# A two-layer transformer kernel: first score maxima between the matmuls of the last projections, and base products interleaved with query and key products in layer 1

## The chip, the cores and the metric

The program runs on one core of one Trainium2 chip. The metric is the device time of one execution in microseconds (us). The engines are named as in the profile: PE (TensorE, matmuls), PEld (its weight loads), DVE (VectorE), ACT (ScalarE), POOL (GpSimd) and SP (SyncE, which here issues all DMA transfers).

## The reference, cut to what matters

Two layers, each with an attention and a feed-forward part that both read the same layer-normed input; everything is f32, x is 2 x 1024 x 512.

```python
xn = layernorm(x)
x = x + L0_attn(xn) + L0_ffn(xn)      # L0_attn: 32 query heads of 16, ONE key and value head, biases
xn = layernorm(x)
x = x + L1_attn(xn) + L1_ffn(xn)      # L1_attn: 32 query heads, 8 key/value heads, rotary, causal
...
def L1_ffn(x):
    w = two largest of softmax(x @ W_router.T), renormalised   # 8 experts
    h = einsum('td,erd->ter', x, lora_A)                        # rank 16
    return x @ W_base.T + b_base + 2 * einsum('ter,eor,te->to', h, lora_B, w)
```

## The kernel before, in words

The 2048 tokens are 16 tiles of 128 (`TT`) or 4 chunks of 512 (`NCH`); the 512 features are 4 blocks of 128 (`KC`). `acc` holds x, `xnT` the transposed normed input. PSUM has eight banks of 128 x 512 (`bank(i)`). All cross-engine order is written out by hand with semaphores: each engine runs its instructions strictly in the order in which the code lists them.

Each layer has, after its feed-forward work, three stages.

**Projections.** 20 products, numbered i = 5c + m: for each chunk c the four query blocks m = 0 to 3 and the key block m = 4 (in layer 0 keys and values together, 32 columns). One product is 4 f32 matmuls of 128 x 512, which the profile counts as 8 records (L1248). ACT copies each product out of PSUM (`q32_ready`) and DVE (in layer 1 both, with the rotary embedding: `rope`, `remainder`, `lowest` on DVE, L954 to L980; `high_roped`, `middle` on ACT) splits it into 2 f32r or 3 bf16 parts. SP stores the parts to memory (`store_parts`, L388) and reads them back in the layout of an attention group (`load_slot`, L400 to L416, 12 transfers into one of 3 slots). In layer 1 the values are 16 further products of 128 x 128, one for each token tile (L1260), after the 20.

**First maxima.** Attention runs over 16 groups of 4 heads. Its softmax subtracts the row maximum, so every group needs a maxima pass: for each item of `max_blocks` PE computes a scores tile into a pair of banks (3-4 or 5-6 in turn; L1346 in layer 0, L1340 and L1343 in layer 1) and DVE reduces it (L1012, L1015); behind the maxima of a chunk a transpose (L1336) hands the chunk's maxima over, negated (L1024, L1026), and SP puts them into the slot as rows (`max_rows`). The maxima of a group run beside the attention of the group before it. Group 0 has no group before it: its first 23 items (`pieces(0, 0, cut(0))`, L1455) run alone, between the projections and the attention.

**Attention.** For each group: scores (L1431, L1427) to PSUM, exponentials on ACT (L752), products with the values (L1401), with the rest of this group's and the first of the next group's maxima in between.

In layer 1 the feed-forward work precedes the projections: `lora_in` (L1184), the gate on DVE (L899 to L933), then `base_product(t)` (L1202, 8 records, into one of 6 banks), the transposed weighted LoRA activations (`hwT`, L1214 on PE, L667 on ACT) and `lora_product(t)` (L1206, 2 records), and DVE adds the bank to `acc` (L937). The projections wait for the last of these (L1226).

## Time and profile before

| | us |
|---|---|
| three runs: lowest, median, highest | 2013.52, 2013.70, 2018.43 |
| the profiled execution's own time | 2015.05 |
| its span on the core | 2013.5 |
| PE busy | 1910.6 (95%) |
| DVE busy | 1379.6 (69%) |
| ACT busy | 1090.0 (54%) |
| mean granted TensorE clock | 0.975 of 2.4 GHz |

Busy times are sums over instructions; matmuls are pipelined and their ends are modelled, so PE can be shown as busy while it waits little or runs at half clock. The share of the whole says little about one stage; the stages are read from stretches of the trace.

### The profile page before, as it was taken

How to read it: one execution, taken by the hardware profiler on the slowest of the kernel's cores; microseconds unless marked ns; L12 is line 12 of the kernel's file. 1: busy time of each engine (PE TensorE's matmuls, PEld its weight loads, DVE VectorE, ACT ScalarE, POOL GpSimd, SP SyncE). 2: the span in 40 equal slices, each digit the busy share in tenths (PEclk: the TensorE clock that was granted, in tenths of full speed). 3: DMA queues.
4: the chain of work that ended last, by engine and by line, in shares of the span. 5: the costliest groups of instructions: out<-in, count | busy, mean ns of one | idle time of the engine just before them, and what ended most of it. 6: DMA issues, size and time to landing. Idle time of an engine off the chain costs nothing.

```text
span 2013.5 us, 29092 instructions
## 1 busy us (share of the span) xinstructions
PE 1910.6 (95%) x10864; PEld 977.8 (49%) x10864; DVE 1379.6 (69%) x1719; ACT 1090.0 (54%) x2177; POOL 231.4 (11%) x606
## 2 busy tenths in 40 slices
PE   6999999998999999999999999999699999999998
PEld 5888887633333333333334346644433333333446
DVE  6554544417899999999897836429677777777733
ACT  3221212232778888788776853204257777677662
POOL 1000000000000001000000100000023433332330
PEclk9999999996999999999999999999879999999999
DMA  6010100042113111122112001002412212212102
GB/s 210 1 48 1 43 1 1 12 143 65 30 37 82 32 31 33 31 49 39 30 31 57 7 7 56 1 0 79 118 25 51 48 32 51 46 34 51 30 10 87
DMA packets 79211, 87.52 MB, mean 43 GB/s; under 512 B 19072, under 2 KB 52864, under 8 KB 79072
## 3 DMA queue, kind: packets, MB, share of 16 engines
q1 hardware_dynamic: 79072, 85.67, 16.9%
q8 instruction: 87, 1.43, 0.3%
q14 instruction: 52, 0.43, 0.1%
HBM read 55.20 MB, written 20.71 MB: 38 GB/s over the span
## 4 chain that ended last, share of the span: by engine, by line
PE 78%; DVE 8%; ACT 7%; SPq 3%; issue 2%; DMA 1%; POOL 0%; DVEq 0%; POOLq 0%; ACTq 0%
PE ps L1401 18%; PE ps L1431 11%; PE ps L1108 8%; PE ps L1109 7%; PE ps L1110 7%; ACT arena L752 6%; PE ps L1427 6%; PE ps L1340 5%; PE ps L1248 4%; PE ps L1346 4%; PE ps L1202 3%; DVE arena L1012 2%; SPq L444 2%; SPq L442 1%; DMA slots<-arena 1%
## 5 line engine op out<-in xcount | busy, mean ns | idle before, releaser
L752 ACT ACTIVATE arena<-ps 128x512 f32<-128x512 f32 (+3 forms) x1792 | 867.4, 557 | 367.5 <-PE ps L1431 188.1
L1012 DVE TENSOR_REDUCE arena<-ps 128x1 f32<-128x1024 f32 (+3 forms) x768 | 855.2, 1153 | 141.8 <-PE ps L1343 66.9
L1401 PE MATMUL ps<-arena 128*17 128x512 f32 (+3 forms) x3584 | 434.9, 557 | 1.0 <-ACT arena L752 0.6
L1346 PE MATMUL ps<-slots 48*128 48x512 f32 x1024 | 410.2, 477 | 9.7 <-DVE arena L1012 8.5
L1431 PE MATMUL ps<-slots 50*128 50x512 f32 x1024 | 384.6, 455 | 22.2 <-ACT arena L752 13.8
L1431 PEld LDWEIGHTS ps<-slots 50*128 50x128 f32 x1024 | 171.2, 187 | 319.8 <-ACT arena L752 273.4
L1427 PE MATMUL ps<-slots 98*128 98x512 bf16 (+3 forms) x768 | 209.3, 331 | 9.7 <-DMA slots<-arena 6.3
L1340 PE MATMUL ps<-slots 96*128 96x512 bf16 (+3 forms) x768 | 199.4, 336 | 16.3 <-DVE arena L1015 8.4
L1346 PEld LDWEIGHTS ps<-slots 48*128 48x128 f32 x1024 | 172.4, 191 | 58.2 <-DVE arena L1012 33.0
L575 POOL TENSOR_SCALAR_AFFINE_SELECT arena<-arena 128x128 f32<-128x128 f32 x512 | 144.4, 292 | 346.6 <-ACT arena L752 338.7
L636 ACT ACTIVATE xn<-ps 128x512 f32<-128x512 f32 (+1 forms) x44 | 26.3, 598 | 260.7 <-PE ps L1110 260.7
L851 DVE TENSOR_TENSOR xn<-xn,ps 128x512 f32<-128x512 f32 (+1 forms) x44 | 30.2, 687 | 166.4 <-ACT xn L636 166.4
L1108 PE MATMUL ps<-x_hi,w_hi 128*128 128x512 f32 (+1 forms) x352 | 138.7, 394 | 5.0 <-DVE x_lo L833 5.0
L1109 PE MATMUL ps<-x_lo,w_hi 128*128 128x512 f32 (+1 forms) x352 | 138.2, 393 | 0.0
L1110 PE MATMUL ps<-x_hi,w_lo 128*128 128x512 f32 (+1 forms) x352 | 138.1, 392 | 0.0
L1427 PEld LDWEIGHTS ps<-slots 98*128 98x128 bf16 x768 | 62.1, 98 | 152.8 <-ACT arena L752 104.6
L1015 DVE TENSOR_REDUCE arena<-ps 128x4 f32<-128x512 f32 (+2 forms) x96 | 97.6, 1044 | 45.0 <-PE ps L1343 45.0
L1401 PEld LDWEIGHTS ps<-arena 128*17 128x17 f32 x3584 | 59.6, 95 | 111.7 <-ACT arena L752 79.3
L1248 PE MATMUL ps<-xnT,w_q 128*128 128x512 f32 x256 | 112.4, 595 | 0.9 <-DVE acc L937 0.9
L1343 PE MATMUL ps<-mask_qk,identb 128*128 128x128 bf16 x512 | 107.7, 224 | 0.0
L1340 PEld LDWEIGHTS ps<-slots 96*128 96x128 bf16 x768 | 70.9, 99 | 71.7 <-DVE arena L1015 19.1
L541 POOL COPY arena<-v_all 128x136 f32<-128x136 f32 x32 | 9.3, 298 | 671.2 <-PE ps L1401 558.2
(127 smaller groups left out, 1851.8 us busy)
## 6 DMA issues: line engine op xcount, KB each, us to landing
slots<-qparts SPq DMA_DIRECT2D x96, 128.0 KB, 3.5
qparts<-arena SPq DMA_DIRECT2D x32, 256.0 KB
xnT<-arena SPq DMA_DIRECT2D x256, 32.0 KB
slots<-qparts SPq DMA_DIRECT2D x96, 64.0 KB, 3.2
qparts<-arena SPq DMA_DIRECT2D x48, 128.0 KB
slots<-qparts SPq DMA_DIRECT2D x32, 192.0 KB, 3.6
w_raw<-in_wgu SPq DMA_DIRECT2D x20, 256.0 KB, 3.2
acc<-in_x SPq DMA_DIRECT2D x4, 1024.0 KB, 7.8
```

The source lines that it names most:

```text
L575: pool.affine_select(out=p, in_=p, compare_op=ALU.is_ge, fill=0.0, base=0, pattern=[[1, P]], channel_multiplier=-1).then_inc(S["p_masked"], 1)
L752: act.activation(prob[local % P_RING][:, q0:CH], bank(local % SP_RING)[:, q0:CH], ACT.Exp, scale=SCALE).then_inc(S["p_ready"], 1)
L1012: dve.tensor_reduce(maxes[c][:, h[0] * TPC + qt:h[0] * TPC + qt + 1], src[:, 0:w], AX_X, ALU.max).then_inc(S["x_done"], 1)
L1108: pe.matmul(out_, hi_w, hi_x, start=start, stop=False)
L1109: pe.matmul(out_, hi_w, lo_x, start=False, stop=False)
L1110: return pe.matmul(out_, lo_w, hi_x, start=False, stop=stop)
L1248: last = pe.matmul(bank(m)[0:wide, :], w, xnT[:, k, c * CH:(c + 1) * CH], start=(k == 0), stop=(k == KC - 1))
L1340: last = pe.matmul(dst[:, k0:k1], q_slot1[u][0:ROWS[1], c, h, qt * P:(qt + 1) * P], k_slot1[u][0:ROWS[1], k0:k1], start=True, stop=k1 < w)
L1346: last = pe.matmul(dst[:, k0:k1], q_slot[u][r:r + ROWS[0], c, h % 2, qt * P:(qt + 1) * P].bitcast(F32R), k_slot[u][r:r + ROWS[0], k0:k1].b ...
L1401: mm = pe.matmul(bank(7)[32 * h:32 * h + DH + 1, q0:CH], v_slot[n % SLOTS][:, kt, :], prob[idx % P_RING][:, q0:CH], start=(kt == 0), stop= ...
L1427: mm = pe.matmul(bank(slot)[:, q0:CH], k_slot1[u][0:ROWS[1] + MROWS, kt * P:(kt + 1) * P], q_slot1[u][0:ROWS[1] + MROWS, c, h, q0:CH], sta ...
L1431: mm = pe.matmul(bank(slot)[:, q0:CH], k_slot[u][r:r + ROWS[0] + MROWS, kt * P:(kt + 1) * P].bitcast(F32R), q_slot[u][r:r + ROWS[0] + MROW ...
```

## The change

It moves work and adds no arithmetic.

1. Layer 0: the 23 first items of the maxima pass are issued on PE one by one between the matmuls of products 12 to 19 (after the 1st, 2nd and 3rd of the four matmuls of each), and DVE reduces them between its other steps of the projections. Products now rotate over banks 0 to 2, value transposes use bank 7 alone.
2. Layer 1: the weights of the feed-forward part are in another place of the arena and so load later (`load_ffn1` waits for `y2_ready`); the base, LoRA and projection work is one sequence: product 0, base 0, product 1, base 1, product 2, base 2, products 3 and 4, and then for each token tile t a transpose of `hw`, LoRA product t, base product t + 3 and query or key product t + 5. DVE and ACT run the rotary and the splits in that order (`ROPES`). Base products rotate over banks 3 to 6, the transposes and the value products share bank 7.
3. Layer 1: the 16 value products come last, and behind each stand one or two of the first 23 items of the maxima pass.
4. SP: stores are unrolled; slot 0 is loaded once its own memory is prepared; slot 1 is loaded before store 13 (layer 0) or 17 (layer 1); the maxima rows of group 0 are written before store 18 (layer 0) or after the last store (layer 1). POOL prepares slots 1 and 2 of layer 1 only after the last LoRA product. ACT waits for the last split instead of the last store before the attention.

```diff
+HWT_RING = 8
+ROPES = [[0, 1], [2], [3, 4], [5], [6, 7], [8], [9, 10], [11], [12], [13], [14], [15], [16], [17], [18], [19]]
+FIRST_MAX_AT = 12
+ROWS_AT = [18, 20]
+LOAD_AT = [13, 17]
...
+def maxima_in_product(i, k, count):
+
+    j = 3 * (i - FIRST_MAX_AT) + k
+    return range(j, j + 1) if i >= FIRST_MAX_AT and k < 3 and j < count else range(0)
+
+
+def maxima_behind_value(t, count):
+    return range(t * count // TT, (t + 1) * count // TT)
+
+
+def product_behind(t):
+
+    return range(KC + 1 + t, KC + 2 + t) if KC + 1 + t < NCH * (KC + 1) else range(0)
...
+                for i in range(QC * NQ, NCH * NQ):
+                    if i == LOAD_AT[l]:
+                        sp.wait_ge(S["v_slot_ready"], SLOTS)
+                        for n in range(1, SLOTS - 1):
+                            load_slot(l, n)
+                    if i == ROWS_AT[l]:
+                        max_rows(l, 0, 0, 0)
+                    store_parts(l, i)
...
-                    sp.wait_ge(L[0]["o_copied"], GROUPS * QC + 1)
+                    sp.wait_ge(L[0]["y2_ready"], TT)
                     load_ffn1()
-                    sp.wait_ge(L[0]["y2_ready"], TT)
...
+                        if u == 1:
+                            pool.wait_ge(S["b_ready"], TT)
...
+                    for i in range(NQ):
+                        whole(i)
+                    copy_hwT(0)
+                    copied = NQ
+                    for t in range(TT):
+                        if t < TT - 1:
+                            copy_hwT(t + 1)
+                        for r in ROPES[t]:
+                            while copied < NCH * NQ and copied < NQ + t and copied <= r + 2:
+                                whole(copied)
+                                copied += 1
+                            split(r)
+                    for t in range(TT):
+                        copy_v(t)
+                        if t < HI_LAG + 1:
+                            split(NCH * NQ + t)
...
+                if l:
+                    for t in range(TT):
+                        for r in ROPES[t][:-1]:
+                            roped(r)
+                        base_evac(t)
+                        roped(ROPES[t][-1])
+                    for t in range(TT):
+                        for j in maxima_behind_value(t, count):
+                            maximum(j, *first[j])
+                        if t < HI_LAG + 1:
+                            roped(NCH * NQ + t)
+                else:
+                    for i in range(NCH * NQ):
+                        for k in range(KC):
+                            for j in maxima_in_product(i, k, count):
+                                maximum(j, *first[j])
+                            if k == 0 and i:
+                                lower(i - 1)
+                        if i >= NQ and i % NQ == 0:
+                            take_v(i // NQ - 1)
...
+                    if i >= 3 and k0 == 0:
+                        pe.wait_ge(S["q32_ready"], i - 2)
...
+                            if piece[0] == 0 and piece[-2]:
+                                pe.wait_ge(S["slot_in"][0], 16 * 12)
+                                pe.wait_ge(*((S["b_evac"], TT) if l else (S["y_evac"], TT * len(ROUNDS) + 1)))
+                            max_piece(*piece)
...
+                    for t in range(TT):
+                        if t < TT - 1:
+                            transpose_hw(t + 1)
+                        lora_product(t)
+                        if t < TT - 3:
+                            base_product(t + 3)
+                        for i in product_behind(t):
+                            product(i)
+                    for t in range(TT):
+                        value_product(t)
+                        first_maxima(maxima_behind_value(t, count))
```

`roped(i)` is `rope(i)`, `remainder(i - 2)` and `lowest(i - 3)`; `split(i)` is `high_roped(i - 2)` and `middle(i - 3)`; `whole(i)` is ACT's copy of product i.

**PE, layer 0, at the end of the projections, before.** The last key product (i = 19), the value transposes (`ident,arena 128x32`) and the first maxima items (`ps<-slots`):

```order
L1248 MATMUL ps<-xnT,w_kv 32x512 [waits q32_ready_0]
L1248 MATMUL ps<-xnT,w_kv 32x512 x3
L1235 MATMUL ps<-ident,arena 128x32 [waits v_done_0,q32_ready_0]
L1235 MATMUL ps<-ident,arena 128x32 x3
L1346 MATMUL ps<-slots 128x512 [waits v_done_0,q32_ready_0,v_slot_ready_0,slot_in0_0]
L1346 MATMUL ps<-slots 128x512 x3
L1346 MATMUL ps<-slots 128x512 [waits x_done_0]
```

**The same engine now, in product 12** (`xnT,w_q` is a quarter of the product, `ps<-slots` twice is one item):

```order
L1435 MATMUL ps<-xnT,w_q 128x512 [waits q32_ready_0]
L1362 MATMUL ps<-slots 128x512 [waits y_evac_0,slot_in0_0]
L1362 MATMUL ps<-slots 128x512
L1435 MATMUL ps<-xnT,w_q 128x512
L1362 MATMUL ps<-slots 128x512 x2
L1435 MATMUL ps<-xnT,w_q 128x512
L1362 MATMUL ps<-slots 128x512 [waits x_done_0]
```

The wait for slot 0 (`slot_in0_0`) stood behind all products and their value transposes; now it stands behind the first quarter of product 12, and three quarters of that product and seven products are queued behind it.

**PE, layer 1, the feed-forward part before** (`ident,arena` is the transpose for `hwT`, L1206 the LoRA product, `arena,xnT` a base product):

```order
L1214 MATMUL ps<-ident,arena 128x128 [waits hwT_sb_1,hw_done_1]
L1206 MATMUL ps<-arena 128x512 [waits hwT_sb_1]
L1202 MATMUL ps<-arena,xnT 128x512 [waits b_evac_1]
L1202 MATMUL ps<-arena,xnT 128x512 x3
L1214 MATMUL ps<-ident,arena 128x128 [waits hwT_sb_1,hw_done_1]
```

**Now**, one step of the loop over t, with a query product in it:

```order
L1279 MATMUL ps<-ident,arena 128x128 [waits hwT_sb_1,hw_done_1]
L1283 MATMUL ps<-arena 128x512 [waits hwT_sb_1]
L1273 MATMUL ps<-arena,xnT 128x512 [waits b_evac_1]
L1273 MATMUL ps<-arena,xnT 128x512 x3
L1435 MATMUL ps<-xnT,w_q 128x512 [waits q32_ready_1]
L1435 MATMUL ps<-xnT,w_q 128x512 x3
```

The 20 products stood behind the last of these steps; now 15 of them stand one in each step, and five ahead of step 0.

**PE, layer 1, now, behind the last LoRA product** (`w_kv,xnT` is a value product, `ps<-slots1` and the mask product make up an item):

```order
L1283 MATMUL ps<-arena 128x512 [waits hwT_sb_1]
L1423 MATMUL ps<-w_kv,xnT 128x128 [waits hwT_sb_1]
L1423 MATMUL ps<-w_kv,xnT 128x128 x3
L1356 MATMUL ps<-slots1 128x128 [waits b_evac_1,slot_in0_1]
L1359 MATMUL ps<-mask_qk,identb 128x128
L1356 MATMUL ps<-slots1 128x128
L1359 MATMUL ps<-mask_qk,identb 128x128
```

Two more such pairs end item 0, and the next value product follows, which waits for ACT's copy of the one before out of bank 7 (`v_done_1`). Before, the 16 value products came behind each other and all 23 items behind the last of them.

## Rows read from the trace of the kernel before

**Rows 1.** The page, part 1: busy time and share of each engine.
```profile
PE 1910.6 (95%) x10864; PEld 977.8 (49%) x10864; DVE 1379.6 (69%) x1719; ACT 1090.0 (54%) x2177; POOL 231.4 (11%) x606
```
**Rows 2.** The chain of waits, 440 to 500: start us, us, what.
```profile
448.37 11.86 PE ps L1248 x27
...
465.85 1.24 DVE arena L1012
467.13 1.23 PE ps L1346 x2
```
**Rows 3.** Stretches: us, busy (x instructions) by engine, PEclk, DMA share, GB/s.
```profile
core 0: us, PE busy (x) PEld busy (x) DVE busy (x) ACT busy (x) POOL busy (x), PEclk, DMA share, GB/s
433.69:462.42 28.73, 28.73 (x69) 10.68 (x67) 5.66 (x9) 10.10 (x16) 0.00 (x0) 1.00 0.55 159
462.42:465.12 2.70, 0.43 (x5) 0.35 (x5) 0.81 (x2) 1.25 (x2) 0.31 (x2) 1.00 0.50 140
465.12:493.22 28.10, 23.86 (x45) 10.47 (x46) 24.96 (x23) 1.28 (x1) 0.48 (x2) 0.53 0.25 51
493.22:504.10 10.88, 10.88 (x41) 4.54 (x40) 8.54 (x8) 6.52 (x12) 0.00 (x0) 0.50 0.00 1
...
1350.30:1421.90 71.60, 71.58 (x184) 33.12 (x184) 64.66 (x119) 27.78 (x50) 2.73 (x3) 1.00 0.30 81
1421.90:1434.16 12.26, 0.00 (x0) 0.00 (x1) 12.03 (x22) 6.15 (x12) 0.00 (x0) 0.66 0.46 138
1434.16:1449.30 15.14, 14.37 (x105) 14.21 (x106) 0.51 (x1) 3.95 (x15) 0.33 (x2) 0.83 0.56 161
1449.30:1472.09 22.79, 18.44 (x81) 6.78 (x82) 20.49 (x23) 0.00 (x0) 0.45 (x2) 0.66 0.00 0
1472.09:1480.20 8.11, 7.75 (x39) 4.12 (x41) 5.41 (x8) 3.81 (x8) 2.04 (x7) 0.50 0.06 13
```
**Rows 4.** Timeline, SP's queue around the load of slot 0 in layer 0.
```profile
428.48 0.81 SPq L388 DMA_DIRECT2D kparts<-arena  x2
430.89 0.35 SPq L411 DMA_DIRECT2D slots<-qparts  x1
...
435.95 0.42 SPq L416 DMA_DIRECT2D slots<-kparts  x1
```
**Rows 5.** DMA issues, 428 to 446: KB each, median us to landing.
```profile
slots<-kparts SPq DMA_DIRECT2D x2, 64.0 KB, 3.2
```
**Rows 6.** The chain of waits, 1270 to 1352: six base products, then one LoRA and one base product.
```profile
1278.19 20.87 PE ps L1202 x48
...
1302.60 3.43 PE ps L1202 x8
1306.14 0.86 PE ps L1206 x2
```
**Rows 7.** Timeline: two f32r matmuls of 512 columns in turn at full clock.
```profile
1235.37 0.39 PE L1110 MATMUL ps<-wo_hi,xo_lo 128*128 128x512 f32 x1
1235.59 0.39 PE L1108 MATMUL ps<-wo_hi,xo_hi 128*128 128x512 f32 x1
```
**Rows 8.** Timeline, ACT's copies that end a chunk of a group, layers 0 and 1.
```profile
520.49 0.60 ACT L743 ACTIVATE arena<-ps 128x512 f32<-128x512 f32 x1
541.85 0.60 ACT L743 ACTIVATE arena<-ps 128x512 f32<-128x512 f32 x1
...
1488.15 0.59 ACT L743 ACTIVATE arena<-ps 128x512 f32<-128x512 f32 x1
1507.64 0.59 ACT L743 ACTIVATE arena<-ps 128x512 f32<-128x512 f32 x1
1518.22 0.59 ACT L743 ACTIVATE arena<-ps 128x512 f32<-128x512 f32 x1
```
**Rows 9.** Layer 1's first maxima, DVE's groups from 1449.2 to 1472.3: busy us, mean ns, idle before.
```profile
L1012 DVE TENSOR_REDUCE arena<-ps 128x1 f32<-128x640 f32 (+3 forms) x15 | 14.5, 1006 | 1.6 <-PE ps L1343 1.4
L1015 DVE TENSOR_REDUCE arena<-ps 128x2 f32<-128x768 f32 (+3 forms) x6 | 5.9, 1043 | 15.3 <-PE ps L1343 15.3
```

More of the change, by code:

```diff
@@ L664, in _ @@
                     act.activation(egap, gap, ACT.Exp).then_inc(S["egap_done"], 1)
-                    for t in range(TT):
-                        act.wait_ge(S["hwT_ready"], t + 1)
-                        act.activation(hwT[:, t, :], bank(t % 2)[:, 0:P], ACT.Copy).then_inc(S["hwT_sb"], 1)
                 if l == 0:
@@ L688, in middle, with whole @@
                     act.activation(part1[m][:, 1, :], rest[m], ACT.Copy).then_inc(S["mid_done"], 1)
-                for i in range(NCH * NQ):
+                def whole(i):
                     c, m = divmod(i, NQ)
-                    rows = 2 * DH if (m == KC and l == 0) else P
                     if c:
@@ L706, in _ @@
[L706 to L712 removed]
+                        high(i, src, bias if m < KC else bias_kv[0:DH, 0:1])
+                        act.activation(q32[m][0:rows, :], src[0:rows, :], ACT.Identity, bias=bias).then_inc(S["q32_ready"], 1)
+                    else:
+                        act.activation(q32[m], src, ACT.Copy).then_inc(S["q32_ready"], 1)
@@ L1204, in lora_product, with transpose_hw @@
+                    def transpose_hw(t):
+                        pe.wait_ge(S["hw_done"], t + 1)
+                        if t:
+                            pe.wait_ge(S["hwT_sb"], t)
+                        pe.transpose(bank(7)[:, 0:P], hw[:, t, :], ident[:, :]).then_inc(S["hwT_ready"], 1)
                     def lora_product(t):
                         pe.wait_ge(S["hwT_sb"], t + 1)
-                        pe.matmul(bank(2 + t % 6), hwT[:, t, :], w_lb, start=False, stop=True).then_inc(S["b_ready"], 1)
@@ L1253, in _ @@
-                if l == 0:
-                    transpose_v(NCH - 1)
-                for t in range(TT if l else 0):
-                    if t >= 3:
-                        pe.wait_ge(S["v_done"], t - 2)
-                    for k in range(KC):
-                        last = pe.matmul(bank(5 + t % 3)[:, 0:kw], xnT[:, k, t * P:(t + 1) * P], w_kv[:, k, kw:2 * kw],
-                                         start=(k == 0), stop=(k == KC - 1))
-                    last.then_inc(S["v_ready"], 1)
-                pe.wait_ge(S["v_done"], V_STEPS[l])
@@ L1264, in _ @@
-                pe.wait_ge(S["q32_ready"], NCH * NQ)
+                        pe.matmul(bank(3 + t % 4), hwT[:, t % HWT_RING, :], w_lb, start=False, stop=True).then_inc(S["b_ready"], 1)
+                pe.wait_ge(S["wp_in"], 16 * (6 if l == 0 else 3))
                 causal = l == 1
```

235 lines of the change are left out of this document (120 added, 115 removed).

## The prediction

> **What bounds the kernel now.** I read the page's busy times first, then the chain of waits, then stretches of the trace, and last the timelines at the places that the change touches. PE is busy 95% of the span and DVE 69% [rows 1], so PE is the bound on the whole; the whole, though, hides two stages in which it is not. The chain of waits shows the first: from 465.85 it goes DVE, PE, DVE, PE in pieces of 1.24 and 1.23 us [rows 2]. That is group 0's first maxima pass in layer 0, 23 items in 28.10 us, with PE at 0.53 of its clock and nothing for it to do but this [rows 3]. The same pass in layer 1 takes 22.79 us at a clock of 0.66, and ahead of it lie 12.26 us in which PE has no instruction at all and 15.14 us for 13 of the 16 value products [rows 3]. The 12.26 us are DVE's: it is busy 12.03 of them with the rotary and splits, which it could not finish beside the 20 products, and ACT cannot copy values out before them. The reader is to see in the table of stretches one column after the other: who is busy, and what clock PE was granted.
>
> The granted clock matters too. It is 1.00 to 465, 0.50 in 493.22 to 504.10, when attention has already begun and PE is busy throughout, and 0.50 again in 1472.09 to 1480.20 [rows 3]. What that costs is read from ACT's copies: in layer 0 a chunk lasts 21.36 us [rows 8], four of its 32 exponentials come before the copy, so from a group's first score to its first copy a warm PE needs about 21.4 + 2.7 = 24.1 us; here it took 520.49 - 493.22 = 27.3. Loss 3.2 us. In layer 1 the short chunk lasts 10.58 us for 16 exponentials [rows 8], so 10.6 + 2.6 = 13.2 against 1488.15 - 1472.09 = 16.1: loss 2.9 us.
>
> **The sum, layer 0.** Until product 12 nothing on PE changes but bank numbers; a product waits for the copy of the one three before, which is two products (6.9 us) old, so I cost it nothing. Product 12 starts at 433.69, and today attention starts 59.5 us later, at 493.22 [rows 3]. Now:
> - The first quarter of product 12, 0.86 us (a product is 3.43 us [rows 6], as all of 128 x 512 in f32), to 434.55.
> - A new wait, for slot 0. Its 12 transfers are issued after the stores of product 9, from 430.89 on, the last at 435.95, and land 3.2 us after issue [rows 4, 5], so near 439.4. The change lets it start no earlier. PE stands for about 5 us, with seven and three quarter products queued behind it. This wait lies on the path.
> - 31 quarters, 26.6 us, and one set of value transposes, 0.9.
> - 22 items of two f32r matmuls at full clock, 0.22 to 0.23 us apart [rows 7], so 0.45 each, and a transpose: 10.0 us. DVE needs 1.27 us an item (28.10 us less start, over 22) and 0.6 for a split, 4.4 us for each product with three items; PE needs 3.43 + 1.35 = 4.8. So DVE keeps up by 0.4 us a product and costs nothing; if its items took 1.4 us it would be the bound.
> - The clock. 5 us of idle PE are more than it had before the fall at the end of the products today (the three lines of 462 to 493 [rows 3]), so it falls. With dense work behind, the nearest case is 1434.16 to 1449.30: mean 0.83, so a third of 15.14 us at half clock. I take 4 us at half, 2.0 lost; bounds 0 and 5.
>
> That is 439.4 + 26.6 + 0.9 + 10.0 + 2.0 = 478.9 for the end of product 19, and as today 2.7 us [rows 3] of copy, transposes, split and slot copy: attention starts at 481.6 instead of 493.2. **Gain 11.6 us.** Those 2.7 us with 0.43 of PE work are the same as today's, and the clock fell behind them today; I therefore take attention to start cold as now and add nothing. Warm, it would add 3.2.
>
> **The sum, layer 1.** The later weight loads cost nothing: they are issued where today's rotary tables are, ahead of them, some 8 us before the first LoRA matmul needs the small two; were they late by a few us, all of it would be on the path. From 1278.19, the start of the base products [rows 6], PE has 36 products of 3.43 (123.5), 16 LoRA products of 0.86 [rows 6] (13.8) and 16 transposes of 0.1 (1.7), and a new wait at step 0: product 4 ends, ACT copies it and the first transpose, about 1.1 us. End 1418.3. Today's 20 products end within 1 us of that, since they were PE-bound too: the interleaving alone gains nothing on PE. What it buys is DVE's time. The 20 rotary sets cost DVE 64.66 + 12.03 us [rows 3], 3.8 each, and now have 125 us to lie in, beside 16 additions of 0.7. In a step of 7.8 us (0.1 + 0.86 + 3.43 + 3.43) DVE does 0.7 + 3.8, or 8.3 in the four steps with two sets; it is never more than a step behind. So at 1418.3 only set 19 and the last splits remain: the last addition to 1419.3, set 19 to 1423.2. The 12.26 us are gone.
>
> Then the value products and the maxima. PE has 16 x 0.9 = 14.4 us of values (13 in 15.14 us at 0.83 of the clock [rows 3]) and maxima of 18.44 us at 0.66, so at most 12.2 warm [rows 3]. DVE has 14.5 + 5.9 + 1.2 (the last falls outside those rows) [rows 9] + 0.6 for the transposed item, 22.2, and 3.2 of leftover splits, from 1423.2: 1448.6 at the earliest. The two are close. At the start ACT's second value copy is queued behind a split that waits for DVE in set 19; PE stands 1421.4 to 1423.5, and about 3 us more for DVE until 1431. The clock probably falls there, but while PE waits for DVE a slow PE costs little; I add 1 us. PE ends about one item ahead of DVE: attention starts at 1449.7 instead of 1472.1. **Gain 22.4 us.** By then PE has run almost without a gap, nearest to the rows before 1421.90 at 1.00, so I take attention to start warm: **2.9 us** more.
>
> SP: slot 1's 12 transfers (5.5 us by the pace of [rows 4]) move ahead of store 13, where no one waits for that store but SP; in layer 1 ahead of store 17, after POOL's memsets behind the last LoRA product, so 1420 to 1425.5, and stores 17 to 19 follow to 1432.5, the maxima rows to about 1438. All are ahead of 1449. The cover is 11 us; a later start of these would go on the path.
>
> 11.6 + 22.4 + 2.9 = 36.9. The profiled execution took 2015.05; that gives 1978.2. It stood 1.35 above the median of the runs, 2013.70, so against the median **1976.8**, which I round to 1977. Bounds: layer 0 from 8.6 (5 lost to the clock) to 16.8 (no loss, warm start); layer 1 from 17 (3 us of further waits, 2.4 of clock, cold start) to 27. Together 25.6 to 43.8: 1970 to 1988.
>
> **Rivals.**
> - *The clock does not hold behind the values.* In the first maxima pass today it fell although PE was busy, and stayed at half (0.66 over 1449.30 to 1472.09 [rows 3]). The small waits for DVE and for the one bank 7 would do it again: PE would need 28.8 + 24.4 = 53 us for values and maxima, attention would start at 1471 and cold. Layer 1 gains 1, the whole 12.6: **2001**. Against it: a PE at half clock would be busy without a gap, and such stretches with f32 work got the clock back (1434.16 to 1449.30). The Trainium skill, "TensorE: Matmul & The Clock Gate", section "A second HAM failure mode: psum-queue depth-cycling", says that small pauses between groups of matmuls that cycle through PSUM banks make the clock oscillate; by that rule this change does harm, and the sum would be 2001. The trace agrees for one dense mix only. Chance 0.11.
> - *Layer 0 gives little.* Slot 0 lands later, among the stores, or DVE becomes the bound between the quarters. Gain 2 instead of 11.6: **1986 to 1988**. Against it: the queue was the same in rows 4. Chance 0.11.
> - *Slower.* ACT runs strictly in order: its copy for the next `hwT` stands behind a split that waits for DVE, whose set stands behind the addition that waits for the LoRA product, which waits for that copy. If this closes into one chain, a step lasts 0.86 + 0.7 + two sets of 3.8 + three ACT copies of 0.6 = 11.0 us instead of 7.8, 15 steps give 48 us, and the time is 2013.7 - 36.9 + 48 = **2025**. It decides from a step of 10.3 us on. Against it: only four steps have two sets, and `high_roped` lags by two products. Chance 0.03.
> - *It doesn't do what it says*: the waits leave values and maxima in series as today: within 0.3%, 0.02.
>
> **How the numbers follow.** The forecast has 0.73, the rivals 0.11, 0.11, 0.03 and 0.02. 1977 is the likeliest case. The range takes in its bounds and the second rival, 1969 to 1990; what is left out is the first rival, the last two and a tail, under 0.2. A difference of 0.3% (6 us) is about what a measurement of this kernel can tell from none. Faster 0.95, same 0.02, slower 0.03.
>
> **What would show it.** In layer 0: a wait of 4 to 6 us on PE for a slot transfer behind the first quarter of product 12, a clock of 0.5 behind it, DVE's reductions 1.6 us apart and not 1.27, and attention starting near 482. In layer 1: steps of 7.8 us, products ending near 1407 (all of layer 1 lies 11.6 earlier), no PE gap of 12 us, attention near 1438 and its first copy 13 us later. It is wrong if attention in layer 0 starts after 488, if steps last over 8.5 us, or if values and maxima take over 35 us.

## The result, and the profile after

| | before | changed |
|---|---|---|
| median of 20 runs, us | 2019.38 | 1996.54 |
| lowest, highest | 2006.74, 2031.62 | 1984.01, 2013.84 |
| profiled execution, us | 2015.05 | 2006.20 |
| its span | 2013.5 | 2004.5 |

The ratio of the changed kernel to the kernel before is 0.9895, with a 95% interval of 0.9872 to 0.9919: faster by 1.05%, some 21 us. One of the changed kernel's 20 runs (2013.84) was in the slower of the two states that a kernel shows, and the ratio leaves it out. The forecast was 1977 against 2013.70, a ratio of 0.982. The direction was right, the size was not, and the time lies outside the range.

The page's busy times hardly move (compare [rows 1]); the work is the same:

```profile
PE 1914.6 (96%) x10864; PEld 975.3 (49%) x10864; DVE 1379.2 (69%) x1719; ACT 1088.6 (54%) x2177; POOL 232.4 (12%) x606
```

What the change touched is in the stretches. These are the changed kernel's, with the columns of [rows 3]: products to the first quarter of product 12, PE's stop, items and products at half clock, the same at full clock, the step into attention and its first 11 us; then layer 1: base, LoRA and product steps, first values, values with items, and the first 8 us of attention.

```profile
core 0: us, PE busy (x) PEld busy (x) DVE busy (x) ACT busy (x) POOL busy (x), PEclk, DMA share, GB/s
390.49:434.45 43.96, 43.96 (x107) 17.28 (x105) 8.93 (x15) 14.66 (x24) 3.00 (x3) 1.00 0.38 113
434.45:439.02 4.57, 0.00 (x1) 0.00 (x0) 0.00 (x0) 0.50 (x1) 0.00 (x0) 0.92 0.71 146
439.02:462.40 23.38, 23.38 (x30) 7.34 (x30) 8.54 (x8) 2.53 (x4) 0.00 (x0) 0.50 0.42 105
462.40:495.90 33.50, 33.50 (x82) 10.80 (x81) 23.60 (x25) 6.31 (x10) 0.00 (x0) 1.00 0.27 73
495.90:498.66 2.76, 0.44 (x5) 0.32 (x4) 0.81 (x2) 1.42 (x3) 0.35 (x2) 1.00 0.47 145
498.66:509.54 10.88, 10.01 (x46) 4.11 (x46) 7.45 (x7) 7.88 (x15) 0.44 (x2) 0.69 0.05 15
1294.18:1434.43 140.25, 139.41 (x337) 61.90 (x337) 92.80 (x231) 33.40 (x72) 0.95 (x1) 1.00 0.17 50
1434.43:1437.95 3.52, 3.23 (x33) 2.86 (x31) 3.45 (x7) 1.83 (x4) 1.84 (x2) 1.00 0.24 72
1437.95:1467.43 29.48, 26.50 (x180) 20.38 (x179) 24.71 (x31) 6.41 (x19) 0.53 (x3) 0.88 0.32 92
1467.43:1475.54 8.11, 6.75 (x55) 3.44 (x53) 6.54 (x9) 5.00 (x12) 3.18 (x12) 1.00 0.12 33
```

Three things are to be seen. PE stands 4.57 us in layer 0, the wait that the forecast named. Behind it the clock is at half for 23.38 us although PE is busy in all of them. And even at full clock 33.50 us pass until the products end at 495.90; the first scores come at 498.66, where 481.6 was forecast and 493.22 was the time before. The forecast had called itself wrong if they came after 488. In layer 1 the 140.25 us of the interleaved steps are as forecast, and the gap of 12.26 us in which PE had nothing to do is gone.

ACT's copies tell what each stage got. First copy of layer 0 and of layer 1 in the changed kernel, to be held against 520.49 and 1488.15 in [rows 8]:

```profile
524.64 0.60 ACT L797 ACTIVATE arena<-ps 128x512 f32<-128x512 f32 x1
1481.13 0.59 ACT L797 ACTIVATE arena<-ps 128x512 f32<-128x512 f32 x1
```

With the last copy of layer 0 (1219.64 before, 1235.67 now) and that of layer 1 (1977.71 and 1970.21) the span splits into five pieces:

| us | before | changed | gain |
|---|---|---|---|
| start to first copy of layer 0 | 520.5 | 524.6 | -4.1 |
| to the last copy of layer 0 | 699.1 | 711.0 | -11.9 |
| to the first copy of layer 1 ("layer 1's stage" below) | 268.5 | 245.5 | 23.0 |
| to the last copy of layer 1 | 489.6 | 489.1 | 0.5 |
| to the end | 35.8 | 34.3 | 1.5 |

So layer 1 brought all of the gain and layer 0's part lost. The 11.9 us in the second line are no work of the change. Nearly all chunks last 21.4 us in both kernels; in the changed kernel's profile two of the last six last 38.9 and 32.7, with the clock at half for 41 us between 1073 and 1114, where before they last 28.9 and 25.9. Three kernels below have the changed kernel's layer 0 order, and the first of these chunks lasts 28.9, 28.9 and 30.2 in them. Of all fourteen below eleven have 28.3 to 30.2 for it and three have 38.9 (one of the eleven then has 35.4 and 38.2 for the next two). This alone makes single executions differ by 10 us or more. It is probably a good part of why the profiled pair differs by 8.9 us and the medians by 22.8, and it is why I read stages below rather than whole times. The 20 runs of the kernel before spread over 1.2%, more than the 0.3% that the forecast took from three.

Layer 1's stage has a spread of its own. Eleven of the profiled kernels have the changed kernel's layer 1 order: their stage takes 241.3 to 245.5 us. Up to 2.6 us of this lies ahead of the sequence of products (56.0 to 58.6 us from the last copy of layer 0 to its first matmul). From that first matmul to the first copy they take 185.3 to 187.0 us: 186.9 or 187.0 in the six whose clock fell for 6.8 us among the values and maxima, 185.3 to 185.5 in the five where it fell for 3.4 us or not at all. So this fall costs 1.6 us, and it is this narrower time that I compare between layer 1 orders.

### The profile page after: what moved, and what is told of

Read it like the earlier page. It is cut to its first block, busy times and chain, and to the rows that moved or that the text cites. A ratio compares the mean times of both kernels' runs of the same rounds, so it can differ in the third digit from the quotient of the medians.

```text
span 2004.5 us, 28840 instructions
## 1 busy us (share of the span) xinstructions
PE 1914.6 (96%) x10864; PEld 975.3 (49%) x10864; DVE 1379.2 (69%) x1719; ACT 1088.6 (54%) x2177; POOL 232.4 (12%) x606
## 4 chain that ended last, share of the span: by engine, by line
PE 81%; ACT 7%; DVE 4%; SPq 4%; issue 2%; DMA 2%; POOL 0%; DVEq 0%; POOLq 0%; ACTq 0%; PEldq 0%
PE ps L1498 19%; PE ps L1528 11%; PE ps L1179 8%; PE ps L1180 7%; PE ps L1181 7%; PE ps L1435 7%; ACT arena L806 6%; PE ps L1524 6%; PE ps L1356 5%; PE ps L1362 4%; PE ps L1273 3%; SPq L468 2%; SPq L466 1%; DMA slots<-arena 1%; DVE arena L1043 1%
## 5 line engine op out<-in xcount | busy, mean ns | idle before, releaser
L1362 PE MATMUL ps<-slots 48*128 48x512 f32 x1024 | 409.7, 474 | 8.8 <-DMA slots<-kparts 4.6
L1356 PE MATMUL ps<-slots 96*128 96x512 bf16 (+3 forms) x768 | 193.6, 328 | 13.8 <-DVE arena L1046 7.7
L1362 PEld LDWEIGHTS ps<-slots 48*128 48x128 f32 x1024 | 171.8, 190 | 66.7 <-DVE arena L1043 22.9
L1435 PE MATMUL ps<-xnT,w_q 128*128 128x512 f32 x256 | 125.5, 629 | 0.4 <-ACT arena L632 0.4
```

The lines of the kernel that those rows point to most:

```text
L1356: last = pe.matmul(dst[:, k0:k1], q_slot1[u][0:ROWS[1], c, h, qt * P:(qt + 1) * P], k_slot1[u][0:ROWS[1], k0:k1], start=True, stop=k1 < w)
L1362: last = pe.matmul(dst[:, k0:k1], q_slot[u][r:r + ROWS[0], c, h % 2, qt * P:(qt + 1) * P].bitcast(F32R), k_slot[u][r:r + ROWS[0], k0:k1].b ...
L1435: last = pe.matmul(bank(i % 3)[0:wide, :], w, xnT[:, k, c * CH:(c + 1) * CH], start=(k == 0), stop=(k == KC - 1))
```

## Experiments

All times from the trace are microseconds from the span's start. The first product starts within 0.7 us of 390.3 in every kernel, so ends of the products and first copies of layer 0 can be compared as they stand, to 1 us.

### One part alone

The changed kernel with layer 0's items behind the products again:

```diff
-    j = 3 * (i - FIRST_MAX_AT) + k
-    return range(j, j + 1) if i >= FIRST_MAX_AT and k < 3 and j < count else range(0)
+    return range(0)
...
                     transpose_v(NCH - 1)
+                    first_maxima(range(count))
```

> Undoes the layer 0 part: the 23 first items stand behind all 20 products again, on PE and DVE; layer 1 as changed. Theory: layer 0's part gains nothing or loses (first copy of attention 524.64 in the changed kernel, 520.49 before), and the whole gain is layer 1's. Then the first copy of layer 0 is near 520.5 again, from the first product of layer 1's sequence to its first copy 187 us as in the changed kernel (210 before), and the run is 23 to 27 us below the kernel before, a few us below the changed one. Rival: layer 0's part does gain some 10 us on the median and only the profiled execution hid it; then this kernel is slower than the changed one by that.

Measured: ratio 0.9893 (0.983 to 0.9956), against the changed kernel's 0.9895; first copies at 517.83 and 1460.38, layer 1's stage 245.4. So the layer 0 part brings nothing that the ratio can tell: taken out, the gain stays, within an interval of some 13 us to either side. The profiles are sharper: with the layer 0 part the first copy comes 6.8 us later. (Against the kernel before it was 4.1; there the clock stayed at half until 504.2, here until 499.3.) The pass itself is as in [rows 3], the second and third stretch here being the maxima and the start of attention:

```profile
390.00:462.00 72.00, 71.84 (x174) 27.97 (x172) 14.95 (x24) 24.09 (x39) 3.00 (x3) 1.00 0.50 142
462.00:491.70 29.70, 24.19 (x49) 10.94 (x50) 25.73 (x25) 1.89 (x3) 0.79 (x3) 0.55 0.08 28
491.70:505.00 13.30, 12.99 (x63) 5.78 (x61) 10.91 (x10) 9.43 (x18) 0.00 (x0) 0.71 0.00 1
```

### Layer 0: the clock

First the stop is taken away, by starting when slot 0 has landed:

```diff
-FIRST_MAX_AT = 12
+FIRST_MAX_AT = 14
-    j = 3 * (i - FIRST_MAX_AT) + k
-    return range(j, j + 1) if i >= FIRST_MAX_AT and k < 3 and j < count else range(0)
+    j = 4 * (i - FIRST_MAX_AT) + k
+    return range(j, j + 1) if i >= FIRST_MAX_AT and j < count else range(0)
```

(`ROWS_AT` for layer 0 follows to 19.)

> Starts the items one by one at product 14 instead of 12, one behind each of the four quarters, so that slot 0 has landed (439.0) before PE reaches its wait (441.4). Theory: the clock fell for the 4.6 us in which PE stood for slot 0; without them it stays at 1.00 through the products. With items of 0.66 us and quarters of 1.05 us next to them: 440.6 + 6 products 20.6 + 22 items at 0.45 + 23 x 0.41 for the switches + 0.7 = 481 for the end of the products, first scores 484, first copy 508, 12 us before the kernel before. Rival: the alternation itself brings the clock down to 0.5; then the products end at 493 or later and the first copy is after 518.

```profile
390.68:441.56 50.88, 50.88 (x123) 20.09 (x121) 10.30 (x17) 17.25 (x28) 3.00 (x3) 1.00 0.43 119
441.56:481.10 39.54, 38.59 (x96) 12.61 (x95) 30.59 (x31) 7.64 (x13) 0.00 (x0) 1.00 0.43 118
```

The clock is 1.00 through the same alternation, the products end at 480.1 (481 expected; the last 1.0 us of the second stretch is PE's wait behind them), the first scores come at 483.91. The first copy was at 512.59, later than the 508 expected, since the clock fell in the step into attention and stayed at half for 17 us. Ratio 0.982 (0.9757 to 0.9882), median 1978.4.

Then the stop is put back without items behind it (`pe.wait_ge(S["slot_in"][0], 16 * 12)` after the first quarter of product 12, items from 14 on):

> The start at 14, with the changed kernel's wait for slot 0 put back behind the first quarter of product 12; between the wait and the items lie one and three quarter products without items. PE idles 4.5 us again and the clock falls near 438.5. If the half clock lasts as long whatever follows, it comes back at 462, 24 us later as in the changed kernel, and the products end near 497. If it was the alternating work that kept it down, the plain f32 products bring it back sooner, by 450, and the products end near 490. If idling isn't what brings it down, the clock stays at 1.00 and they end at 485.5.

PE's row behind the stop, and the stretches from it on:

```profile
438.32 8.73 PE L1435 MATMUL ps<-xnT,w_q 128*128 128x512 f32 x14 [4.69 <-DMA slots<-kparts]
```

```profile
439.00:446.00 7.00, 7.00 (x12) 2.83 (x11) 0.69 (x1) 1.27 (x2) 0.00 (x0) 0.69 0.32 118
446.00:486.50 40.50, 40.50 (x100) 12.94 (x98) 30.26 (x31) 7.59 (x12) 0.00 (x0) 1.00 0.38 98
```

The clock did fall, for 6.8 us by the trace's clock record (436.5 to 443.3, 1.8 us of it still in the stop), and was back before the first item at 448.0; the products ended at 486.5, a little earlier than the 490 expected of a quick recovery. The same stop with items directly behind it had cost 23.9 us of half clock by the same record (438.3 to 462.2). So the stop brings the clock down, and the items behind it keep it down. The changed kernel's layer 0 order is in three more of the kernels below: there the half clock lasted 23.9, 23.9 and 13.7 us, so this is a habit of the order and not of one execution. The short recovery with plain products was profiled once.

How short a stop is enough? The start at 13 has one:

```diff
-FIRST_MAX_AT = 14
+FIRST_MAX_AT = 13
```

> The start one by one with four items a product, at product 13 instead of 14: PE reaches the wait for slot 0 at 438.0, and the last transfer lands at 439.0, so PE stands 1 us. It tells whether so short a stop already costs the clock. Theory: it took 4.6 us of idle PE before; 1 us is hidden, the clock stays at 1.00, and the products end at 481, as with the start at 14. Rival: the clock falls, and behind it the items keep it at half for 24 us; the end is near 492.

```profile
437.40:438.92 1.52, 0.01 (x2) 0.01 (x1) 0.00 (x0) 0.50 (x1) 0.00 (x0) 1.00 0.52 142
438.92:440.40 1.48, 1.48 (x4) 0.59 (x4) 0.72 (x1) 0.00 (x0) 0.00 (x0) 1.00 0.52 184
440.40:495.00 54.60, 54.60 (x76) 16.77 (x75) 24.99 (x26) 5.04 (x8) 0.00 (x0) 0.50 0.25 69
```

I had expected nothing of it. The stop was 1.5 us, the clock fell 1.9 us behind its end, and PE then worked 54.6 us at half clock, busy all the time; the products ended at 506.2, later than even the rival's 492, the first copy came at 539.31, and the run took 2022.4. Two kernels tell whether the stop did this. One has the same order with the first item two quarters later (`j = 4 * (i - 14) + k + 2`), so that PE doesn't stop; the other has the wait alone at product 13 and the items from 14 on.

> One item behind each quarter as in the start at 13, but the first behind the third quarter of product 13 (439.7), when slot 0 has landed (439.0), so PE doesn't stop. In the start at 13 PE stood 1.0 us, the clock fell at 440 and stayed at half for 55 us. If that stop of 1.0 us was the cause, the clock here is 1.00 to the end of the products, near 481. If the items cost the clock when they begin this early, or by chance, it falls here too and the end is after 490.

> The start at 14 with PE's wait for slot 0 put behind the first quarter of product 13, where it lasts 1.0 us; behind it three plain quarters before the first item. If a stop of 1.0 us is enough to bring the clock down, it falls near 440 here too; if the plain quarters then bring it back it is up again by 450 and the end is at 484 to 486, if the items keep it down for long the end is after 490. If three plain quarters behind the stop are enough for it not to fall, the end is at 482.

Without the stop, items from 439.89 to the end of the products:

```profile
439.89:480.30 40.41, 40.38 (x100) 13.21 (x99) 30.88 (x31) 7.57 (x12) 0.00 (x0) 1.00 0.41 117
```

With the stop and plain quarters behind it, the stop, the quarters, the items:

```profile
437.21:438.52 1.31, 0.00 (x1) 0.00 (x1) 0.69 (x1) 0.49 (x1) 0.00 (x0) 1.00 0.47 117
438.52:442.27 3.75, 3.75 (x9) 1.20 (x9) 0.00 (x0) 0.82 (x2) 0.00 (x0) 1.00 0.52 186
442.27:480.80 38.53, 38.53 (x96) 12.61 (x95) 30.26 (x31) 6.75 (x11) 0.00 (x0) 1.00 0.40 107
```

Both hold 1.00 to the end of the products, at 480.3 and 480.8 (481 and 482 expected). So neither the early items nor a short stop alone cost the clock; the short stop with items behind it did. Each of the three was profiled once, and the stop without items was 0.2 us shorter, so whether it would each time stays open.

In both kernels the clock then fell in the step into attention and stayed at half for 20.5 us: first copies 513.41 and 514.78, though their first scores came at 483.06 and 484.64. Every profiled kernel has the clock at half somewhere in this step, for 6.8 to 20.5 us in most, and the time from first scores to first copy is 25.4 to 30.4 us with it. First copies therefore carry some 5 us of chance that first scores do not.

### Layer 0: what an item costs

The chain of waits of the changed kernel at full clock, an item (L1362) and a quarter of a product (L1435) in turn:

```profile
469.54 0.66 PE ps L1362 x2
470.20 1.05 PE ps L1435 x2
```

I had taken 0.45 and 0.86. Both are 0.2 us longer, 0.41 for each item. Two more runs tell the number format from the shape, on the order of the start at 14. In the first the items multiply 128 rows, in the second they are f32 like the products but keep their 48 rows.

```diff
+                        if j < count:
+                            last = pe.matmul(dst[:, k0:k1], k_slot[u][:, 0:P].bitcast(F32R),
+                                             k_slot[u][:, k0:k1].bitcast(F32R), start=True, stop=True)
+                        else:
```

> As the start at product 14 one by one, but the 23 first items multiply 128 rows (all rows of the slot's keys with themselves, in place of 48 rows of queries and keys), still f32r; so group 0's first maxima are of other numbers and the row sums of group 0 differ. It tells what makes a quarter 1.05 instead of 0.86 us and an item 0.66 instead of 0.45. If it is the change of row geometry (48 rows at an offset after 128 rows at 0), the quarters take 0.86, the items 0.44 and the products end near 472. If it is the change of number format (f32 to f32r and back), nothing changes: 1.05 and 0.66, end near 480.

The chain, first behind the 32-column key product, then behind a 128-column query product:

```profile
444.74 0.67 PE ps L1362 x2
445.40 0.97 PE ps L1439 x2
446.38 0.66 PE ps L1362 x2
447.04 0.86 PE ps L1439 x2
447.90 0.46 PE ps L1362 x2
448.36 0.86 PE ps L1439 x2
```

```diff
+                        t = F32 if j < count else F32R
-                        last = pe.matmul(dst[:, k0:k1], q_slot[u][r:r + ROWS[0], c, h % 2, qt * P:(qt + 1) * P].bitcast(F32R),
+                        last = pe.matmul(dst[:, k0:k1], q_slot[u][r:r + ROWS[0], c, h % 2, qt * P:(qt + 1) * P].bitcast(t),
...
```

> As the start at 14 one by one, but the 23 first items are f32 matmuls (4 records' worth of time: 2 x 0.86 us instead of 2 x 0.22), on the same 48 rows. If the format change costs, there is none here: quarter 0.86, item 1.72, 2.6 us for both, products end near 500. If the row geometry costs, the quarter stays at 1.05 and the item is 1.93: 3.0 us for both, products end near 509.

```profile
452.20 1.05 PE ps L1436 x2
453.25 1.91 PE ps L1363 x4
```

Format is out: items in f32 leave the quarter at 1.05 and take 1.91, 0.19 above 4 x 0.43, and the products end at 507.7 (509 expected of shape, 500 of format). Shape decides: with 128 rows against 128 x 128 weights the extra vanishes at the row where the products turn from 32 to 128 columns, 0.86 and 0.46, and f32r changes with f32 for nothing (with the 32-column products it stays, so the products ended at 474.4 and not at 472). The timelines show how: in the changed kernel (first two lines) the weight load behind a change starts together with its matmul; with items of 128 rows (third line) it starts at 446.65, under the item before, for the quarter that starts at 447.04.

```profile
468.42 0.30 PEld L1435 LDWEIGHTS ps<-xnT,w_q 128*128 128x128 f32 x2 [0.37 <-issue]
468.42 1.12 PE L1435 MATMUL ps<-xnT,w_q 128*128 128x512 f32 x2
446.65 0.42 PEld L1439 LDWEIGHTS ps<-xnT,w_q 128*128 128x128 f32 x2
```

The Trainium skill, "TensorEngine Tiling (Array Packing)", section "Key Properties", has the rule: a change of tiling mode drains TensorE. The trace agrees with it by the late weight load and by the price: 48 rows against 128, or 32 columns against 128, cost 0.1 to 0.2 us each way. I had not weighed it in the prediction.

Fewer changes, then: items in pairs behind the second and fourth quarter (`return range(j, min(j + 2, count)) if i >= FIRST_MAX_AT and k % 2`, with `j = 4 * (i - 14) + k - 1`).

> As the start at product 14, but the items stand in pairs behind the second and the fourth quarter of a product: 12 places instead of 23. If each change between a quarter and items costs PE 0.2 us, in both directions, this saves 11 x 0.41 = 4.5 us against the start at 14 one by one: products end near 476.5, first copy 503.5. If DVE decides (5.6 us of reductions and split for a product, two items in a row 2.5 us), nothing is saved and PE waits for DVE in the middle of the pairs.

```profile
457.27 1.91 PE ps L1435 x4
459.18 0.67 PE ps L1362 x4
459.85 1.91 PE ps L1435 x4
461.76 1.26 PE ps L1362 x4
```

The first scores come at 476.77, 7.1 us before those of the start at 14 one by one (6.2 if one takes off that the first product starts 0.9 us earlier here), where 4.5 were expected; first copy 503.6, as expected. The last product ends at 473.1, the last item behind it at 473.8. **Median 1973.6, ratio 0.9775 (0.9728 to 0.9821).** The surprise is the pair of 0.67 us: four matmuls in the time of two and a change. The heads stand in the order 2, 0, 3, 1, so the two of a pair read slot rows from 64 and from 0. (Every second pair takes 1.26, since its second item waits for DVE: DVE gets through four reductions and a split in 5.75 us, 2.9 for a pair, where PE alone would come round in 2.6.)

```diff
-        return [(h,) for h in (2, 0, 3, 1)]
+        return [(h,) for h in ((2, 0, 3, 1) if causal else (2, 3, 0, 1))]
```

> The pairs at 14, with layer 0's heads taken in the order 2, 3, 0, 1 instead of 2, 0, 3, 1, so that both items of a pair read slot rows at the same offset (64 and 64, 0 and 0) instead of at 64 and 0. With the pairs at 14 a pair whose banks are free takes 0.67 us for four matmuls of 512 columns, of which each alone takes 0.22. Theory: matmuls in the two halves of the rows run beside each other, two at a time; in the same rows they take 4 x 0.22 + 0.22 = 1.1 us, and the products end up to 2.6 us later (six of the twelve pairs are held by DVE anyway). Rival: 0.67 is how the ends of matmuls are modelled; then it stays at 0.67.

```profile
457.60 1.11 PE ps L1362 x4
458.71 1.91 PE ps L1435 x4
```

1.11 to 1.14 us for each of the first nine pairs, as the theory had it: four matmuls in a row where the two row halves had worked beside each other. The products end at 474.9, 1.8 us later than with the pairs at 14. The order of heads holds for all of layer 0, and its chunks now last 22.5 us instead of 21.4. The one run took 2047.4; some 35 us of the loss are the 32 chunks, and much of the rest falls where the clock was at half, for 51 us from 479 on and for 61 us from 1131 on. Whether the order of heads has to do with these falls was not tested.

### Layer 1: which part of it

Values in one piece and the items behind them, the steps interleaved as changed (on PE `first_maxima(range(count))` behind the loop over `value_product(t)`, on DVE the last `roped` ahead of all maxima):

> Layer 1 with the base and projection steps interleaved as changed, but the 16 value products in one piece and the 23 items behind them, as before. Theory: of the 23 us that layer 1 gained, the interleaving gives what DVE's rotary backlog cost (12.3 us of PE idle) and the overlap of values and maxima the rest. The values take 15 us, the maxima 22.8 as before (DVE and a clock of 0.5 to 0.66), so from the first product of layer 1's sequence to its first copy 187 + 8 (5 in series, 3 for the cold start) = 195 us. Rival: the maxima are DVE-bound either way, and it is no more than 190.

Layer 1's stage was 263.8 us, 18.4 more than the changed kernel's, and 205.3 us from first product to first copy; ratio 1.0022 (0.9987 to 1.0058). Neither theory had that. PE's rows show it: each value product now waits for ACT's copy out of the one bank 7, most of them 1.53 us apart, and the 16 took 27.7 us (the kernel before had three banks for them).

```profile
1437.03 1.16 PE L1422 MATMUL ps<-w_kv,xnT 128*128 128x128 f32 x8 [0.38 <-ACT v_all L750]
1438.57 1.16 PE L1422 MATMUL ps<-w_kv,xnT 128*128 128x128 f32 x8 [0.37 <-ACT v_all L750]
```

So the run undid one thing and laid bare another. The same with four value banks in turn:

```diff
+V_BANKS = [7, 0, 1, 2]
...
-                        last = pe.matmul(bank(7)[:, 0:kw], xnT[:, k, t * P:(t + 1) * P], w_kv[:, k, kw:2 * kw],
+                        last = pe.matmul(bank(V_BANKS[t % 4])[:, 0:kw], xnT[:, k, t * P:(t + 1) * P], w_kv[:, k, kw:2 * kw],
```

> Layer 1's values in one piece and the 23 items behind them, as in the run with the maxima in series, but with the values in four banks in turn (7, 0, 1, 2), so that they needn't wait for ACT's copy of bank 7. There the 16 values took 27.7 us. Theory: half of that run's loss of 18 us was this bank; now the values take 16 us and the stage from the last copy of layer 0 to the first of layer 1 is 264 - 11 = 253 us, still 8 above the changed kernel's 245.4. Rival: DVE's remaining rotary sets hold ACT's copies, and it is 258 or more.

Stage 251.6, where 253 was expected, and 193.0 us from first product to first copy: the single bank had cost 12.3 us. But for one value bank more this is layer 1 as before with the interleaved steps alone. The kernel before took 1488.15 - 1278.19 = 210.0 us from its first base product to the first copy, so the steps bring 210.0 - 193.0 = 17.0 by themselves.

Next, all base and LoRA steps first and the 20 products behind them, values and items in turn as changed (`product_behind` unused; DVE does all `base_evac`, then all `roped`; ACT all `copy_hwT`, then copies and splits):

> Layer 1 with all base and LoRA steps first and the 20 products behind them as before, but values and maxima in turn as changed. Theory: DVE's rotary backlog is back, PE idles near 12 us at the end of the products and DVE starts the maxima that much later: from the first base product to the first copy 187 + 12 = 199 us. Rival: DVE's backlog lies beside the value products, and only the maxima wait for it: under 193.

197.3 us from first base product to first copy, where 199 was expected, stage 253.3, ratio 0.9949 (0.9918 to 0.998). DVE's backlog is back, as PE's wait behind item 0 (four pieces of one item, then the next value product):

```profile
1433.61 2.08 PE L1418 MATMUL ps<-w_kv,xnT 128*128 128x128 f32 x8 [10.47 <-ACT v_all L750]
```

The turns of values and items alone bring 210.0 - 197.3 = 12.7 (the stage shows 15.2, but 2.5 of that lie ahead of the first base product). Both parts together bring 23.0 in the changed kernel, less than the sum of 29.7.

### A faster version

The pairs of layer 0 one place earlier (`j = 4 * (i - 14) + k + 1`, from product 13), the four value banks, and six values ahead of the first item:

```diff
-    return range(t * count // TT, (t + 1) * count // TT)
+    u, n = t - VALUES_FIRST + 1, TT - VALUES_FIRST + 1
+    return range(u * count // n, (u + 1) * count // n) if u >= 0 else range(0)
```

> The pairs at 14, with every pair one place earlier (the first behind the last quarter of product 13), and in layer 1 the value products in four banks in turn (7, 0, 1, 2), the first six of them without an item behind, the 23 items behind the other eleven. Layer 0: first copy 0.7 to 1 us earlier than with the pairs at 14 (503.6). Layer 1, theory: in the changed kernel PE stands for ACT's copy of bank 7 and for DVE's last rotary in the first items (1437.8 to 1442.5), the clock falls for 6.8 us, and DVE then sets the end: with no such stop the first scores follow DVE, 22.2 us behind its last rotary; from the last copy of layer 0 to the first of layer 1 241.5 us instead of 245.4. Rival: PE alone sets the end (values 14.4 + items 12.2 + changes of tile), and it stays at 244 to 246. The whole: 1969 to 1972, ratio 0.975.

```profile
1394.60:1400.00 5.40, 5.40 (x31) 3.79 (x30) 5.30 (x11) 2.43 (x5) 1.84 (x2) 1.00 0.30 90
1400.00:1427.15 27.15, 23.90 (x187) 18.05 (x186) 25.66 (x32) 5.97 (x19) 0.78 (x3) 1.00 0.38 106
```

Layer 1's stage is 239.6, 5.9 below the changed kernel's, but 2.4 of that lie ahead of the sequence, where nothing differs. From its first matmul to the first copy it takes 183.6 us, against 185.3 to 187.0 in the eleven kernels with the changed order: the four banks and the six values ahead are worth 1.7 us against those whose clock hardly fell and 3.4 against the changed kernel itself. Which of the two brings it was not tested. The clock is at 1.00 and DVE busy 25.66 of 27.15 us (PE 23.90), which fits the theory that DVE sets the end. With them both parts of layer 1 together bring 26.4. In layer 0 the earlier pairs gained next to nothing (first scores 476.76, as with the pairs at 14); that the first copy came 0.8 us earlier, as expected, is a shorter fall of the clock in the step into attention. Median 1972.8, ratio 0.9799 (0.9763 to 0.9836), where 1969 to 1972 and 0.975 were expected. The intervals of this and of the pairs at 14 overlap; both are below the changed kernel's 0.9895, and which is the better one isn't settled.

| kernel | first scores, layer 0 | first copy, layer 0 | layer 1's stage | its sequence to first copy | ratio |
|---|---|---|---|---|---|
| before | 493.2 | 520.5 | 268.5 | 210.0 | 1 |
| changed | 498.7 | 524.6 | 245.5 | 187.0 | 0.9895 |
| layer 0 in series | 491.7 | 517.8 | 245.4 | 186.9 | 0.9893 |
| start at 14 | 483.9 | 512.6 | 241.3 | 185.3 | 0.982 |
| pairs at 14 | 476.8 | 503.6 | 245.4 | 186.9 | 0.9775 |
| pairs at 13, four value banks | 476.8 | 502.8 | 239.6 | 183.6 | 0.9799 |

## Why the prediction was right or wrong

**What bounds the kernel, and PE's wait for slot 0: right.** PE stood 4.57 us (5 forecast), with the release at 439.02 (439.4).

**The clock behind it in layer 0: the step that failed.** "With dense work behind, the nearest case is 1434.16 to 1449.30 ... I take 4 us at half, 2.0 lost; bounds 0 and 5." Measured were 23.38 us at half. An item and a quarter took 1.15 + 2.00 there and 0.66 + 1.06 at full clock, so by this estimate 10.6 us were lost.

```profile
440.24 2.00 PE ps L1435 x2
442.25 1.15 PE ps L1362 x2
```

The fall was foreseen; its length was taken from value products of 128 x 128, and this work is another mix. With plain products behind the same stop it lasts 6.8 us. The bound of 5 came from one row of another stage and was no bound.

**22 items "0.45 each": mis-sized.** The forecast priced an item by [rows 7], which is the pace of two matmuls of the same shape behind each other, and had no term for the change from one shape to another. Between quarters an item costs 0.66 and makes its quarter 1.06: 0.86 in all, 9.4 us more over 23 items. "DVE keeps up" was right, and with a wider margin than forecast, since PE became slower. The two terms together are 8.6 + 9.4 = 18 us, less 0.4 for the slot, where 17.0 were missing: the products ended at 495.9 and not at 478.9. The second rival ("layer 0 gives little") came nearest to the outcome, with wrong causes: slot 0 was not late and DVE was not the bound.

**The step into attention: right.** 2.76 us (2.7), and a cold start: the clock is 0.69 over its first 11 us, first copy 26.0 us behind the first scores (27.3 cold, 24.1 warm).

**Layer 1, steps: right.** 140.25 us from the first product to the first value (140.1), steps of 7.84 us, no wait longer than the one at step 0, the later weight loads hidden. DVE was less than a step behind: set 19 and its remainder were done at 1439.5, 5.1 us behind the end of the products, where 4.9 were forecast.

**Layer 1, values and maxima: right in size.** 33.0 us to the first scores (31.4). The stops at the start are those foreseen, ACT's value copy behind a split, and DVE:

```profile
1439.83 1.16 PE L1423 MATMUL ps<-w_kv,xnT 128*128 128x128 f32 x8 [1.80 <-ACT v_all L750]
...
1442.53 0.50 PE L1356 MATMUL ps<-slots 96*128 96x384 bf16 x1 [1.10 <-DVE arena L1046]
```

The clock fell at 1441.8, in the second of them, for 6.8 us and came back among the values and items: 0.88 over that stretch. The first copy came 13.7 us after the first scores, warm as forecast (13.2). Layer 1 gave 23.0 of the 25.3 us forecast. The rival of a clock that stays at half there (2001) did not come. It drew on the Trainium skill's rule on depth cycling through PSUM banks ("TensorE: Matmul & The Clock Gate", section "A second HAM failure mode: psum-queue depth-cycling"). The runs bear it out little: with this order of values and items and its small waits the clock fell for 6.8 us in six profiled kernels, for 3.4 us in three and not at all in two, and with four value banks it held 1.00 over 27.15 us with PE waiting 3.25 of them. The split of the gain I had wrong: the interleaving brings 17.0 alone and the turns 12.7, where I counted the gap of 12.26 and some 10. Each also hides part of what the other does, and the one bank for 16 values takes part of it back: with four banks and six values ahead the sequence is 1.7 to 3.4 us shorter.

**Slower, and no effect:** neither came; no step lasts over 7.9 us.

Sum by the profiled pair: layer 0 gave -4.1 instead of 11.6, layer 1 23.0 instead of 25.3 with the warm start. 19 us are the change's own, against the 21 of the timed ratio.

## What to carry over

Work of a few hundred ns put between large matmuls costs no more than its own time only if it has their shape. Price each change of row or column shape on TensorE (here 0.2 us, both ways) before interleaving, group such pieces so that there are fewer changes, and let neighbours of a group sit in different row halves, where they run beside each other. And start interleaved work only when its input has surely landed: a stop of PE costs more than itself, here 6.8 us at half clock with plain products behind it and 14 to 24 us with items between them. Shifting the start by two products turned a loss of 5 us at the first scores into a gain of 9, and pairing the items made it 16. Last, before a gain of a few us is credited to a change, see how much the same stage differs between executions in which nothing of it was changed: here 4 us in layer 1's.

## What was not expected of the hardware

- The same alternation of quarters and items held the clock at 1.00 for 38 to 40 us where it began without a stop, and at 0.50 for 23.9 us in three kernels and 13.7 us in one (4.57 us of stop in the changed kernel) and 54.6 us in one (1.5 us of stop) where it began directly behind one, with PE busy in every us. The work that keeps a clock up was slow to bring it back up.
- Four f32r matmuls of 48 rows took 0.67 us with their rows at 64 and 0, and 1.11 us with both items of the pair at the same offset. In whole chunks of attention this order of heads is worth 21.4 against 22.5 us.
- Matmuls of f32 and f32r follow each other at no cost (0.86 and 0.46 us). Matmuls of 128 and 48 rows cost 0.2 us at each change (1.05 and 0.66), and of 32 and 128 columns 0.1 to 0.2 (0.97 and 0.66).
